# Graph network kernel: loads interleaved, weight preparation between the first sum's blocks, first graph's check moved to the end

## The reference, cut to what matters

```
h = x                                    # (8, 1024, 128)
for i in range(4):
    hw = einsum('bnc,cd->bnd', h, weight[i])
    m  = einsum('bjn,bjd->bnd', adj, hw)
    gx, gh = m @ w_ih[i].T + b_ih[i], h @ w_hh[i].T + b_hh[i]     # three parts each: r, z, n
    r, z = sigmoid(xr + hr), sigmoid(xz + hz)
    n = tanh(xn + r * hn)
    h = (1 - z) * n + z * h
out = layernorm(x + h * mask[:, :, None])
```

## Time and profile before

| | |
|---|---|
| median of three runs | 546.95 us (546.69 to 547.09) |
| profiled execution, own time | 549.29 us |
| its span | 547.5 us |
| busy share of the span | PE 94%, PEld 77%, DVE 73%, ACT 69%, POOL 40% |
| moved by DMA | 80.93 MB, mean 148 GB/s |

### The profile page before, as it was taken

One profiled execution on the slowest core, in us unless ns is written; L12 is line 12 of the kernel. 1 busy time (PEld: TensorE's weight loads), 2 busy tenths in 40 slices (PEclk: granted clock), 3 DMA queues, 4 the chain that ended last, 5 costly groups with the idle time before them and its releaser, 6 DMA issues.

```text
span 547.5 us, 7461 instructions
## 1 busy us (share of the span) xinstructions
PE 515.9 (94%) x2288; PEld 420.4 (77%) x2288; DVE 397.9 (73%) x695; ACT 375.4 (69%) x616; POOL 218.8 (40%) x161
## 2 busy tenths in 40 slices
PE   5898999999999999999999999999999999999950
PEld 4566888888888888788888888888888788888740
DVE  3997767666689786666699886666779886666666
ACT  2855777747786787875886877874886677664422
POOL 0034344443245554333345644233354545244332
PEclk9999999999999999999999999999999999999995
DMA  7952256164662165373662156365472122323302
GB/s 225 389 215 77 88 210 222 53 179 136 199 222 78 62 227 196 109 215 117 196 248 75 59 209 214 111 187 158 134 270 81 55 77 78 116 93 123 108 25 80
DMA packets 79808, 80.93 MB, mean 148 GB/s; under 512 B 3656, under 2 KB 63648, under 8 KB 79776
## 3 DMA queue, kind: packets, MB, share of 16 engines
q1 hardware_dynamic: 79504, 80.41, 44.6%
q10 hardware_dynamic: 272, 0.13, 0.1%
HBM read 60.08 MB, written 20.45 MB: 147 GB/s over the span
## 4 chain that ended last, share of the span: by engine, by line
PE 78%; DVE 9%; DMA 5%; issue 3%; ACT 3%; SPq 2%; POOL 1%; DVEq 0%; ACTq 0%; POOLq 0%
PE p_S L472 34%; PE p_r L482 5%; PE p_r L486 5%; PE p_r L483 5%; PE p_z L482 5%; PE p_z L486 5%; PE p_z L483 5%; PE p_hn L482 2%; PE p_hn L483 2%; PE p_hn L486 2%; PE p_xn L486 2%; PE p_xn L482 2%; PE p_xn L483 2%; DMA bounce<-work 2%; DMA adj_in<-in_adj_dram 2%
## 5 line engine op out<-in xcount | busy, mean ns | idle before, releaser
L1256 POOL TENSOR_TENSOR work<-hT,work 128x512 f32<-128x512 f32 x63 | 87.5, 1390 | 259.8 <-ACT work L676 259.8
L472 PE MATMUL p_S<-adj_hi,nat_hi 128*128 128x512 f32 x480 | 187.4, 391 | 0.0
L472 PE MATMUL p_S<-adj_hi,nat_lo 128*128 128x512 f32 x480 | 186.8, 389 | 0.0
L472 PEld LDWEIGHTS p_S<-adj_hi,nat_hi 128*128 128x128 f32 x480 | 90.1, 188 | 18.9 <-DVE nat_lo L848 0.3
L472 PEld LDWEIGHTS p_S<-adj_hi,nat_lo 128*128 128x128 f32 x480 | 90.1, 188 | 18.5
L1137 DVE SCALAR_TENSOR_TENSOR work<-p_hn,bias,work 128x512 f32<-128x512 f32 x62 | 46.5, 749 | 79.4 <-ACT work L676 79.2
L1260 POOL TENSOR_TENSOR work<-work 128x512 f32<-128x512 f32 x63 | 90.4, 1434 | 4.9
L676 ACT ACTIVATE work<-p_r,bsum 128x512 f32<-128x512 f32 x63 | 43.3, 687 | 63.2 <-PE p_r L486 61.9
L676 ACT ACTIVATE work<-work,bias 128x512 f32<-128x512 f32 x63 | 45.7, 726 | 41.5 <-DVE work L1141 36.2
L905 DVE STREAM_TRANSPOSE work<-hT 128x512 f32<-128x512 f32 x62 | 69.1, 1114 | 2.1
L621 ACT ACTIVATE adj_hi<-adj_in 128x1024 fp32r<-128x1024 f32 x60 | 60.3, 1050 | 0.5 <-DMA adj_in<-in_adj_dram 0.4
(11 more groups left out here) (148 smaller groups left out, 925.6 us busy)
## 6 DMA issues: line engine op xcount, KB each, us to landing
adj_in<-in_adj_dram SPq DMA_DIRECT2D x64, 512.0 KB, 6.3
bounce<-work SPq DMA_DIRECT2D x62, 256.0 KB, 2.0
low<-bounce SPq DMA_DIRECT2D x62, 256.0 KB, 2.8
x_in<-in_x_dram SPq DMA_DIRECT2D x8, 512.0 KB, 6.7
y<-in_x_dram SPq DMA_DIRECT2D x8, 512.0 KB, 4.3
out_dram<-y SPq DMA_DIRECT2D x7, 512.0 KB, 4.1
y<-in_L_gnn_w_ih_dram SPq DMA_DIRECT2D x2, 192.0 KB, 3.4
y<-in_L_gnn_w_hh_dram SPq DMA_DIRECT2D x2, 192.0 KB, 4.3
```

The source lines that it names most:

```text
L472: last = nc.tensor.matmul(p_S[h][:, :], part[:, s, j], adj_hi[:, s, j, half(h)], start=(j == 0 and part is nat_hi), stop=(j == NB - 1 and ...
L1256: nc.gpsimd.tensor_tensor(t_sb[:, h], hT[:, s, half(h)], n_sb[:, h], ALU.subtract).then_inc(d_sub, 1)
```

## The change

The loads go x, layer 0's weights, adjacency blocks 0 and 1, layer 1, blocks 2 and 3, and so on, the small rows ahead of the last two blocks. The gate weights are read with three rows of one gate matrix in a partition, `(p q) d`, so in pieces of 1536 bytes instead of 512; `by_gate` and `by_block` put the columns back in order in the copies out of PSUM. Preparation of layer 0 stands before the first sum, that of the others between its blocks: transposes after block 1, 3 and 5, the join after block 2, 4 and 6. Even blocks of the first two graphs are cast by ScalarE, odd ones by VectorE. VectorE's check of graph 0 is gone; graph 0 is loaded once more in the last pair, and ScalarE checks it there. The long diff is cut to its core:

```diff
-        p_start = [(p_r, p_z), (p_S[0], p_S[1]), (p_hn, p_xn), (p_r, p_z)]
+        p_start = [(p_r, p_z), (p_hn, p_xn), (p_r, p_z), (p_hn, p_xn)]
...
+        def by_gate(t):
+            return t.rearrange("c (p q) -> c q p", q=G)
+        def by_block(t):
+            return t.rearrange("c (q p) -> c q p", q=G)
...
-                sp.dma_start(w_nat[l][:, 1:1 + G], w_ih[l].rearrange("(q p) d -> p q d", p=P)).then_inc(w_in[l], 16)
+                sp.dma_start(w_nat[l][:, 1:1 + G], w_ih[l].rearrange("(p q) d -> p q d", p=P)).then_inc(w_in[l], 16)
...
+            sp.dma_start(x_in[:, 0], x_v[0]).then_inc(x_loaded[0], 16)
             for l in range(L):
                 load_layer(l)
+                if l == L - 1:
+                    load_rows()
+                for j in (2 * l, 2 * l + 1):
+                    sp.dma_start(adj_in[:, j], adj_v[0, j]).then_inc(adj_loaded[j], 16)
             sp.dma_start(x_in[:, 1], x_v[1]).then_inc(x_loaded[1], 16)
             for j in range(NB):
-                wait_adj(sp, 0, j)
-                sp.wait_ge(adj_checked, j + 1)
+                wait_adj(sp, 0, j, True)
                 sp.dma_start(adj_in[:, j], adj_v[1, j]).then_inc(adj_loaded[j], 16)
...
                     if g in (2, 3):
-                        if not last:
-                            next_adj(p, 0, first, range((g - 2) * HB, (g - 1) * HB))
+                        next_adj(p, 0, first, last, range((g - 2) * HB, (g - 1) * HB))
...
             transpose_weights(0)
-            transpose_weights(1)
-            join_weights(0)
-            transpose_weights(2)
-            join_weights(1)
-            transpose_weights(3)
-            join_weights(2)
-            transpose_x(0, 0, True)
-            join_weights(3)
-            pe.wait_ge(start_lo, 2)
+            transpose_x(0, 0, True)
+            join_weights(0)
...
+                        if s == 0 and 1 <= j < NB - 1:
+                            l_next = (j + 1) // 2
+                            if j % 2:
+                                transpose_weights(l_next)
+                            else:
+                                join_weights(l_next)
...
-                copy(wh_hi[:, l], p_start[l][1][:, 0:G * C])
+                copy(by_gate(wh_hi[:, l]), by_block(p_start[l][1][:, 0:G * C]))
...
-                checks = [(p, 1, j) for j in range(NB)] + [(p + 1, 0, j) for j in range(NB) if not last]
+                checks = [(p, 1, j, first, False) for j in range(NB)]
+                checks += [(p + 1, 0, j, False, last) for j in range(NB)]
...
-                        places = ((), (0,), (2, 4), (6,)) if first else ((4, 5), (6,), (7,), ())
+                        places = ((0,), (2,), (4,), (6,)) if first else ((4, 5), (6,), (7,), ())
...
+            split_x(0, 0, True)
             split_w_hh(0)
+            take_adj(0, 0, 0, True)
+            take_xT(0, 0)
+            split_joined(0)
+            for l in range(1, L):
+                take_adj(0, 0, 2 * l, True)
+                split_w_hh(l)
+                split_joined(l)
...
+            def take_odd(s, j):
+                dve.wait_ge(adj_loaded[j], 16 * (s + 1))
+                nc.vector.tensor_copy(adj_hi[:, s, j], adj_in[:, j]).then_inc(odd_ready, 1)
...
-            for j in range(NB - 2):
-                check_adj(0, 0, j, True)
+            split_x(0, 0)
+            copy_weights(0)
+            take_odd(0, 1)
             take_xT(0, 0)
+            split_weights(0)
+            for l in range(1, L):
+                copy_weights(l)
+                if l == L - 1:
+                    take_rows()
+                take_odd(0, 2 * l + 1)
+                split_weights(l)
```

More of the change, by code:

```diff
@@ L283, in _, with next_adj @@
             sp.dma_start(x_in[:, 1], x_v[1]).then_inc(x_loaded[1], 16)
             for j in range(NB):
-                wait_adj(sp, 0, j)
-                sp.wait_ge(adj_checked, j + 1)
+                wait_adj(sp, 0, j, True)
                 sp.dma_start(adj_in[:, j], adj_v[1, j]).then_inc(adj_loaded[j], 16)
-            def next_adj(p, s, first, blocks):
+            def next_adj(p, s, first, last, blocks):
                 for j in blocks:
-                    sp.wait_ge(adj_checked, NB * (2 * p + 1 + s) + j + 1)
-                    wait_adj(sp, 2 * p + 1 + s, j, first and s == 0)
-                    sp.dma_start(adj_in[:, j], adj_v[2 * p + 2 + s, j]).then_inc(adj_loaded[j], 16)
+                    if s == 0:
+                        sp.wait_ge(adj_checked, NB * (2 * p) + j + 1)
+                        if first:
+                            wait_adj(sp, 1, j, True)
+                    else:
+                        wait_adj(sp, 2 * p + 2, j)
+                    sp.dma_start(adj_in[:, j], adj_v[0 if last else 2 * p + 2 + s, j]).then_inc(adj_loaded[j], 16)
@@ L768, in body @@
                         h_high(p, g - 1, 1)
+                    if early:
+                        s_high(p, g, 1)
                     if g == 0:
@@ L774, in body @@
                         fill(0)
-                    s_high(p, g, 1)
-                    if early:
-                        fill(1)
+                    else:
+                        s_high(p, g, 1)
                     for h in range(2):
@@ L784, in body @@
                             take_back(p, g - 1, 0)
-                        if h == 1 and not early:
+                        if early:
+                            fill(1 + h)
+                        elif h == 1:
                             fill(1)
@@ L867, in split_x @@
                 lo(nat_lo[:, s], x_in[:, s], nat_hi[:, s]).then_inc(xnat_lo, 1)
-            for l in range(L - 1):
-                copy_weights(l)
-            split_weights(0)
-            split_weights(1)
-            copy_weights(3)
-            nc.vector.tensor_copy(bias[:, :, :].rearrange("p a b -> p (a b)"), p_rows[:, 0:2 * L * G])
-            nc.vector.tensor_copy(mask[:, :], p_rows[:, 2 * L * G:2 * L * G + B * NB]).then_inc(rows_out, 1)
-            split_x(0, 0)
-            split_weights(2)
-            split_weights(3)
-            dve.wait_ge(rows_out, 1)
-            nc.vector.tensor_tensor(bsum[:, :], bias[:, 0], bias[:, 1], ALU.add).then_inc(rows_out, 1)
-            def check_adj(p, s, j, first=False):
-                dve.wait_ge(adj_loaded[j], 16 * (2 * p + s + 1))
-                if not (first and s == 0 and j == 0):
-                    dve.wait_ge(adj_checked, NB * (2 * p + s) + j)
-                nc.vector.tensor_tensor(low[:, :], low[:, :], adj_in[:, j].bitcast(I32),
-                                        ALU.bitwise_or).then_inc(adj_checked, 1)
             def take_xT(p, s):
@@ L1089, in body @@
             def body(p, first, last):
-                checks = [(0, 0, NB - 2), (0, 0, NB - 1)] if first else []
-                def fill():
-                    if checks:
-                        check_adj(*checks.pop(0))
-                        if not checks:
-                            mask_first()
                 for g in range(STEPS):
@@ L1109, in body @@
                         turn(p, g - 1, 1)
-                        if first and g == 1:
-                            take_adj1(7)
                     elif not first:
@@ L1119, in body @@
                         h_low(p, g - 1, 1)
+                    if first and g == 0:
+                        s_low(p, g, 1)
                     if g == 0:
@@ L1123, in body @@
                         split_x(p + 1, 0)
-                    fill()
-                    s_low(p, g, 1)
+                    if not (first and g == 0):
+                        s_low(p, g, 1)
                     if not first:
```

106 lines of the change are left out of this document (41 added, 65 removed).

## The result

| | before | changed |
|---|---|---|
| median of eight runs | 548.66 us (546.69 to 548.90) | 542.48 us (541.93 to 545.03) |
| ratio to before | | 0.9904, 95% interval 0.9884 to 0.9925 |
| profiled execution, span | 549.29 us, 547.5 us | 542.58 us, 540.5 us |
| TensorE's busy share | 94% | 95% |

A forecast was written before the change was run, and what follows sets the result against it. TensorE bounds the loop from 60 us; only the head can gain. 2.1 us from an earlier start plus 5.0 of stalls, less 0.3 for small waits, is 6.8: 546.95 - 6.8 = 540.2 us, range 538.9 to 543.2 (forecast's own 539.0 to 541.2).

The forecast's parts named there:

- What bounds the kernel: From 60 us the loop is TensorE's; before that, 5.0 us of idle between the gates of steps 0 and 1.
- Part 3: Between the gates of steps 0 and 1: check off VectorE, blocks cast in turns; 5.0 us of stalls go.
- Part 4: Last pair: the first graph's load and 8 checks, 8.4 us on ScalarE, are covered by other work; cost zero.
- Part 2: First sum with preparation between its blocks: step 0's gates at 24.3 instead of 26.40, so 2.1 us.
- Part 1: Loads at the start: 1.5 us a layer instead of 2.03; layer 0 lands at 6.2, block 7 at 21.1.
- Strided copies: Weight copies writing SBUF at every third word: taken as no cost; 1.9 us lost kept as the end.
- the end with factor 1.6: Weight copies at 1.6 times the plain copy's time: 4.2 us a layer over 3.5, gates at 26.2, 1.9 lost.
- the prediction's own sign of being wrong: In the head: the prediction counts as wrong if weight copies take over 0.6.
- A: Loads: pieces of 1536 bytes no faster, only stalls won; gates 26.3, gain 4.8 to 5.1, 542.0 us; chance 0.14.
- B: Weight copies: strided writes cost 1.6 times; gain 4.9, 542.0 us; chance 0.15.
- C: Head: TensorE stays at half level, a layer 6.6 instead of 3.5; 2.8 us slower, 549.8; chance 0.04.
- D: Second sum still starves, odd casts waiting behind GpSimd; 5 us would return, no difference; chance 0.02.

The follow-up runs named there:

- tiny_check: Kernel before, with the OR, mask and reduction of VectorE's low-bit check of graph 0 cut to one word a row; 544.39 us, ratio 0.9938.
- casts_and_check_only: Changed kernel with the load order, row order and preparation of before, keeping the new casts and the moved check; 542.80 us, ratio 0.9902.
- changed_3: The changed kernel itself, unaltered, run again in one call with some variants; 542.84 us, ratio 0.9900 to before.
- changed_again: The changed kernel itself, unaltered, run again to see its scatter; 542.32 us, ratio 0.9908 to before.
- rows_512: Changed kernel with gate weights read in the former row order, 512-byte pieces, and contiguous copies out of PSUM; 543.47 us, ratio 0.9914.
- psum_side: Changed kernel with the weights' reordering moved to the PSUM reading side of the copies, SBUF written in order; 541.95 us, ratio 0.9883.
- layer0_first: Changed kernel with x loaded behind layer 0 instead of ahead of it; 543.48 us, ratio 0.9935 to before.
- changed_warm: Changed kernel with 22 transposes of the identity ahead of layer 0's; 541.96 us, ratio 0.9888 to before.

## Why the prediction was half right

- **What bounds the kernel.** Right: TensorE from 60 us on, 497.8 to 499.1 us from gates 1 to the end in every variant (500.0 in the first profile of before); only the head moved.
- **Part 3, the casts and the check.** Right in mechanism and size. Forecast 5.0 us, of the 4.84 that were there 4.6 went (21.07 to 16.40 to 16.46). tiny_check splits it: 2.9 for the check's length, the rest for the order. The times given for blocks 5 and 7 (34.2, 38.1) came at 35.8 and 39.9, of which 1.5 is the later start; the needs moved with them.
- **Part 4.** Right: the checks are under other work. The 1.7 us by which the spans differ beyond the marks weren't theirs.
- **Part 2 is the step that failed.** "24.3. Now it is 26.40, so 2.1 us": measured 25.75 to 26.30 against 25.97 to 26.40, so 0.2 us on the mean, and 0.5 by casts_and_check_only, whose head is the former one. The whole change of loads and preparation, from which 2.1 us were to come, gave almost nothing, and its interleaving by itself came out 0.6 to 1.1 us later in three pairs. In the first profile the pieces are: up to block 1 all fits (12.52 against 12.5). Then 0.68 of waits for blocks 2 and 4, whose landings I had a microsecond too early; 0.2 more for layer 3's transposes; 0.5 more in the tail behind the last join, from the strided writes. That makes 1.4 of the 1.45.
- **Part 2 in the other two profiles.** changed_3 and changed_again have no wait for blocks 2 and 4 and are no earlier (25.83 and 26.30). There TensorE stayed at the pace of the half level (1.2 GHz) until about 12.3 and 13.1 us, as its durations show: the join ahead of the sum took 1.49 in both instead of 0.94, the eight matmuls of blocks 0 and 1 2.90 and 3.15 instead of 2.15. The blocks behind had landed by the time they were needed. From changed_again:

```profile
10.87 1.20 PE L449 MATMUL p_S<-adj_hi,nat_hi 128*128 128x512 f32 x1
11.87 0.63 PE L451 MATMUL p_S<-adj_hi,nat_lo 128*128 128x512 f32 x1
...
14.02 0.49 PE L401 MATMUL p_hn<-ident,hT 128*128 128x128 f32 x3
...
26.30 0.47 PE L488 MATMUL p_r<-hT_hi,wh_hi 128*128 128x512 f32 x1 [1.05 <-DVE wx_lo L855]
```

- **Part 1's landings.** The rate was even better than taken: a layer 1.3 us instead of 1.5. What I missed is a gap at the start. Layer 0 landed at 6.6 and block 0 at 2.82 + 6.0 = 8.8, where 7.5 was forecast:

```profile
4.00:5.00 1.00, 0.00 (x0) 0.00 (x0) 0.00 (x0) 0.40 (x1) 0.00 (x0) 1.00 0.72 153
```

  In this stretch the queue moved 153 GB/s with issued work waiting (205 and 181 in the other two profiles), and block 7 still landed 0.7 later than forecast. Why it does, I did not test.
- **Strided copies.** "I take no cost" was wrong, the end with factor 1.6 too high: 1.39 and 1.28. So the prediction's own sign of being wrong, weight copies over 0.6, came true. The price, 0.3 to 0.5 us, is how much shorter the last wait is in psum_side.
- **Rivals.** A (pieces no faster) is refuted by rows_512. B is half true: strided writes cost, but less than it said. Both had named 542.0 us and gates near 26.3, which is about what was measured; that is luck, for the time was largely lost elsewhere. C (half level kept) came in part: in the two profiles above the level lasted into the sum and cost 1.0 and 1.2 us from the join to the end of block 1, not the 9.9 of the rival. D has nothing for it: the second sum has no wait.

Part 2 can be summed up in three terms, from TensorE's first transpose to the gates. The forecast had a start at 6.2, 17.1 us of work and 1.0 of waits. The three profiles have starts at 6.67, 6.66 and 6.94, work of 17.2, 18.1 and 18.3, and waits of 1.9, 1.05 and 1.05. So every term was taken at its best. In every order tried, TensorE's own work from its first transpose to the gates is 17 to 19 us. Before the change it was 18.5, with 3.4 of waits; a plan that starts TensorE 1.7 us later and wants the gates 2.1 us earlier had to remove all of them and more. Starting early alone isn't the answer either: layer0_first starts at 4.44 and ends where the changed kernel does.

## What to carry to other kernels

When an engine starves, look at what stands ahead of the needed instruction in the supplier's list: 13 us of checks that nobody waited for held casts worth 0.65 us each. Before reordering a start-up phase, sum the bound engine's work from the moment when it can begin; only what is above that sum can be won, and a later start has to be paid from it. When a change has several parts, measure each alone: here one part gave the gain, one gave about 1 us at an early mark and another took a good half of that back. If a reordering must be paid somewhere, try it on the PSUM reading side of the copy before writing SBUF in steps.

## What the runs showed of the hardware

- An instruction that takes 384 words a partition out of PSUM: 0.68 instead of 0.49 us on ScalarE when it writes every third word of SBUF, 0.70 instead of 0.55 on VectorE when it also reads its second operand so; read at every 128th word of PSUM and with SBUF in order: 0.49 and 0.55.
- Weight reads in pieces of 1536 bytes between adjacency blocks: 1.3 us for 448 KB and for a block of 512 KB alike, so about 350 to 400 GB/s; with 512 bytes layer 3 came 1.8 us later.
- VectorE's cast of 1024 words took 1.78 us instead of 0.69 when GpSimd's product ran from 37.65 to 39.31 beside it.
- In changed_warm TensorE was back at the 1.2 GHz level after 2.07 us of idle time that followed 3.95 us of work. In the profiles without the warm-up the page of the profile writes granted clock 1.00 for the first stretch of work although its transposes take the time of the half level.
